# Second layer: the last two score tiles of the next head behind the projection instead of in front of it

## The reference

```python
qkv = xn @ w_qkv                      # x normalised, 256 -> 3 * 16 * 64
q = q * scale
sim = jnp.einsum('bhid,bhjd->bhij', q, k)
attn = jax.nn.softmax(sim, axis=-1)
out = jnp.einsum('bhij,bhjd->bhid', attn, v)
out = out.reshape(b, n, 1024) @ w_out
```

## Time and profile before

| | |
|---|---|
| median of the runs | 3472.14 us |
| the profiled execution | 3466.49 us, its span 3464.7 us |
| mean granted clock of the TensorE | 0.988 |
| busy share: PE, DVE, ACT, POOL | 96%, 72%, 56%, 68% |
| in the chain that ended last | PE 61%, every other engine 1% or less |
| phase B | from about 1239 us to the end |

### The profile page before, as it was taken

One profiled execution on the slowest core, in us unless ns is written; L12 is line 12 of the kernel. 1 busy time (PEld: TensorE's weight loads), 2 busy tenths in 40 slices (PEclk: granted clock), 3 DMA queues, 4 the chain that ended last, 5 costly groups with the idle time before them and its releaser, 6 DMA issues.

```text
span 3464.7 us, 58322 instructions
## 1 busy us (share of the span) xinstructions
PE 3327.1 (96%) x16386; PEld 2701.4 (78%) x16386; DVE 2480.8 (72%) x4709; ACT 1951.3 (56%) x3226; POOL 2359.6 (68%) x2084
## 2 busy tenths in 40 slices
PE   5999999999999969999999999999999999999997
PEld 4877777777777747888888888888888888888886
DVE  6877777777777756766766667667677666776764
ACT  3333333333333347767767777677777777767774
POOL 4666666666666527777777777777777777777776
PEclk9999999999999979999999999999999999999999
DMA  2110011001001032222222222222322222222222
GB/s 78 31 31 28 28 31 31 26 29 31 27 29 31 25 94 59 47 71 63 59 71 56 62 70 50 66 70 46 74 59 59 73 56 60 70 50 66 70 49 53
DMA packets 195099, 180.22 MB, mean 52 GB/s; under 512 B 87955, under 2 KB 155813, under 8 KB 194469
## 3 DMA queue, kind: packets, MB, share of 16 engines
q1 hardware_dynamic: 194980, 179.04, 20.7%
HBM read 77.25 MB, written 34.08 MB: 32 GB/s over the span
## 4 chain that ended last, share of the span: by engine, by line
PE 61%; DMA 1%; ACT 1%; DVE 1%; POOL 1%; issue 0%; SPq 0%; POOLq 0%; ACTq 0%; DVEq 0%
PE psV_b L1342 7%; PE psV_b L1347 7%; PE psS_b L1330 7%; PE psS_b L1329 7%; PE psV_b L1343 7%; PE psN_b L1315 6%; PE psY_b L1270 4%; PE psX_b L1270 4%; PE psY_b L1271 3%; PE psY_b L1272 3%; PE psX_b L1272 3%; PE psX_b L1271 3%; POOL pp_lo_b L1061 1%; PE psN_b L1399 0%; DMA xT_lo<-xT_lo_dram 0%
## 5 line engine op out<-in xcount | busy, mean ns | idle before, releaser
L1061 POOL TENSOR_TENSOR pp_lo_b<-pf_b,pp_hi_b 128x1024 fp32r<-128x1024 f32 x512 | 1227.6, 2398 | 606.6 <-ACT pp_hi_b L1103 518.9
L1206 DVE TENSOR_REDUCE negmax_b<-psN_b 128x2 fp32r<-128x1024 f32 x512 | 627.1, 1225 | 387.8 <-PE psN_b L1315 380.1
L1098 ACT ACTIVATE pf_b<-psS_b 128x1024 f32<-128x1024 f32 x512 | 526.0, 1027 | 239.4 <-PE psS_b L1330 236.2
L692 PE MATMUL psM_a<-wr_hi_a,xt_hi_a 128*128 128x512 f32 x1024 | 439.6, 429 | 48.1 <-DVE acc_a L528 40.1
L1329 PE MATMUL psS_b<-qA_b,kA_b 128*128 128x512 f32 x1024 | 405.6, 396 | 6.3 <-DVE qB_b L1221 4.5
L694 PE MATMUL psM_a<-wr_hi_a,xt_lo_a 128*128 128x512 f32 x1024 | 409.7, 400 | 0.0
L693 PE MATMUL psM_a<-wr_lo_a,xt_hi_a 128*128 128x512 f32 x1024 | 407.8, 398 | 0.0
L1330 PE MATMUL psS_b<-qB_b,kB_b 68*128 68x512 f32 x1024 | 406.4, 397 | 0.0
L1342 PE MATMUL psV_b<-pp_hi_b,vals_hi_b 128*128 128x512 f32 x1024 | 402.9, 393 | 1.4
L1343 PE MATMUL psV_b<-pp_hi_b,vals_lo_b 128*128 128x512 f32 x1024 | 402.3, 393 | 0.0
L1315 PE MATMUL psN_b<-kA_b,qA_b 128*128 128x512 f32 x1024 | 322.8, 396 | 4.8 <-DVE negmax_b L1206 4.1
(11 more groups left out here) (200 smaller groups left out, 7824.1 us busy)
## 6 DMA issues: line engine op xcount, KB each, us to landing
kA_b<-kA_b SPq DMA_DIRECT2D x128, 256.0 KB, 3.2
qB_b<-qA_b SPq DMA_DIRECT2D x128, 256.0 KB, 2.9
inverse_b<-inverse_dram SPq DMA_DIRECT2D x256, 128.0 KB, 3.0
x_a<-x_dram SPq DMA_DIRECT2D x64, 128.0 KB, 2.1
xT_hi_dram<-xrt_hi_a SPq DMA_DIRECT2D x64, 128.0 KB, 2.1
xT_lo_dram<-xrt_lo_a SPq DMA_DIRECT2D x64, 128.0 KB, 2.1
base_dram<-base_a SPq DMA_DIRECT2D x64, 128.0 KB, 1.8
xT_hi<-xT_hi_dram SPq DMA_DIRECT2D x16, 512.0 KB, 4.3
```

Source lines behind the costliest of these rows:

```text
L692: pe.matmul(out, lh, rh, start=start, stop=False)
L1061: pool.tensor_tensor(pp[1][:, c], pf[:, c], pp[0][:, c].bitcast(F32), ALU.subtract).then_inc(pl_pool, 1)
L1098: a.activation(pf[:, c], psS[:], ACT.Exp).then_inc(exp_act, 1)
L1206: v.tensor_reduce(negmax[:, n.slot(2), 2 * c:2 * c + 2], psN[:], AX.X, ALU.max, negate=True).then_inc(mx_dve, 1)
```

## The change

One call of two matmuls is moved on the TensorE's list, in every step: `scores(n, 1)` now stands behind the first projection of the step (queries in an even step, values or output in an odd one), and in front of `weigh(g, 0)`.

```diff
--- before.py
+++ after.py
@@ -1384,12 +1384,12 @@
                     weigh(m, 1)
                 if here:
                     scores_t(g, 1)
-                if n.within(0, NH):
-                    scores(n, 1)
                 if g.const % 2 == 0:
                     kq(g, q_unit(g), 1)
                 else:
                     shared(g)
+                if n.within(0, NH):
+                    scores(n, 1)
                 if here:
                     weigh(g, 0)
                 if n.within(0, NH):
```

## The result

The changed kernel takes 3630.01 us (median of 4 runs, 3628.53 to 3635.32), the kernel before in the same comparison 3472.43 us: 157.6 us more, ratio 1.0459, 95% interval [1.0441, 1.0477]. The forecast was 3600 us, range 3545 to 3670, slower.

The account below looks back on a forecast made before the run. TensorE's own list was taken to bound the head stage. Even 0.60 plus odd 0.47 made 1.07 us a pair, times 125 pairs 134 us, less 2 at the start: 3599, stated as 3600 us, range 3545 to 3670.

Parts of the forecast that it names:

- The mechanism: Head stage: moved pair releases second maximum, cast, low part and `row()` on VectorE, then the next step's first matmul; 3.7% slower.
- The prediction's other signs: Head stage: TensorE near 94% busy at clock 1.00, maxima waiting longer for psN, even casts near 0.9 us.
- The odd steps: Odd steps of the head stage: 0.63 us longer with a values' unit, 0.32 with an output unit, 0.47 on average.
- The wait of mt by itself: Mt waits about 0.2 us for the second maximum, swallowed by the larger wait for `row()`.
- The 1 to 2 us credited at the start: Start of the head stage: the values' projection runs inside the pair's 4.1 us wait for its maxima, gaining 1 to 2 us.
- the prediction's 4.27: Even step: chain from pair to the next step's second matmul takes 4.27 us; the TensorE has 3.59 us for it.
- the even step: Even step of the head stage: 0.68 us longer, 0.48 with the cast clear of GpSimd; taken as 0.60.
- The next instruction starts 0.08 us ahead of a cast's end.: VectorE in the even step: cast ends at 2412.86, next instruction starts at 2412.78, `row()` 0.61 us later.
- Everything up to otf moves forward, so I take 0.6.: Even step after an odd one that waited: ScalarE copies keys earlier relative to the TensorE; 0.6 us taken, not 0.68.
- A: Rival, head stage: only mt waits, 0.2 us a step, 50 us in all, 3517 us; chance 0.12.
- B: Rival, even steps: the cast stands fully behind a late otf, GpSimd's product; 3660 us; chance 0.14.
- C: Rival: not slower if the chain is no longer than the TensorE's 3.59 us; 4.1 us gained, 3468 by median; chance 0.05.

Follow-up runs that it names:

- the half move: Against the kernel before, the pair put between the third and fourth of the projection's six matmuls, three behind its old place; 3548.43 us, 1.0224.

## Why the prediction was right, and where it was off

The mechanism was right: a chain that goes from the pair through `row()` and back, longer than the work that the TensorE has left, and seen as a wait of the first psS matmul in nearly every step. The prediction's other signs came as well: the clock at 1.00, the maxima waiting longer for psN (2.44 us in the step shown, 0.89 before). The odd steps were well sized: by the TensorE's first matmuls they grew from 8.44 to 9.05 us with a values' unit and from 8.49 to 8.78 with an output unit (medians), 0.61 and 0.29 us against 0.63 and 0.32 forecast; over both kinds the mean is 0.42. The wait of mt by itself was put at 0.2 us; it shows alone in odd steps with `row()` first, 8.73 - 8.53 = 0.20 and 8.71 - 8.53 = 0.18 us. The 1 to 2 us credited at the start were 2.5.

That the chain of the step shown is 4.28 us, and the prediction's 4.27, is luck in part: its cast is 0.11 us shorter than forecast (0.77 for 0.88), and the first term below makes up for just that.

What was mis-sized is the even step, forecast at 0.60 us and measured at 0.87. Two terms of it failed:

1. "The next instruction starts 0.08 us ahead of a cast's end." In odd steps that holds (0.60 us behind the start of a cast of 0.68). In front of the query's low part there were 0.03 us behind the end instead, in all 104 even steps between 1500 and 3400 us (0.02 to 0.04). That is 0.11 us a step, 14 us. The trace of before has it, but not in the step that the prediction read: in 99 of 112 even steps there, that one among them, the low part started about 0.1 us behind the cast, right behind a copy of ScalarE. In the other 13 the copy was in time, and it is 1544.65 - (1543.48 + 1.14) = 0.03 us:

```profile
1543.48 1.14 DVE L1216 CAST pp_hi_b<-pf_b 128x1024 fp32r<-128x1024 f32 x1
...
1544.65 0.69 DVE L1195 SCALAR_TENSOR_TENSOR qA_b<-psX_b,qA_b 64x512 fp32r<-64x512 f32 x1
```

2. "Everything up to otf moves forward, so I take 0.6." Otf didn't always. The reciprocal is queued behind `row()` on VectorE; it feeds a DMA to DRAM and two back, and otf waits for these. The prediction listed what is queued behind the cast and left this one out. 32 of 104 otfs waited for the DMA; the casts of these steps are 1.30 us on the mean, those of the other 72 are 0.80. All even casts came to 0.96 us where 0.60 us of excess stood for a cast of about 0.80. That is 0.16 us a step, 20 us. Two kernels show the cause from two sides: with the reciprocal early the casts are 0.73 us and the time falls by 27 us; with otf cut short it falls by 29 us.

0.11 + 0.16 = 0.27 us is the difference of the even step; with 125 steps 34 us, less 6 for the odd steps (0.42 by the TensorE's starts against 0.47), 28 us. The excess was forecast at 134 - 2 = 132 us and measured at 158, 26 us short, so the two terms cover it. The other 4 of the 30 us between 3600 and 3630 are the forecast's own: its sum is 3599 us for the profiled execution, and with the 6 us that it names for the median it would have been 3605.

Of the rivals, A (only mt waits, 3517) fell with the changed kernel itself, and with `row()` first in odd steps, which made these 0.22 us shorter and left mt where it was. B (3660) had otf starting late, and that did happen, but in 32 of 104 steps and for another reason, the wait for the DMA; its longer form of 1.75 us did not come back (the median in the changed kernel is 1.29). C, not slower, holds where its condition holds: with the pair in the middle of the projection and the cast free of GpSimd, the time is that of before.

The cast's wait for GpSimd is what the Trainium skill ("SBUF — State Buffer", Who interferes with whom) states as an exclusive lock. The runs here agree: a cast that started inside a GpSimd product and had to wait ended 0.54 to 0.56 us behind that product's end, from 0.77 to 1.61 us long in the rows shown. The one of 1.61 us had run beside the product for 1.07 us and was then no nearer to its end than the one of 0.77 us, which had waited 0.22.

## What to carry to other kernels

When a step is moved on the engine that bounds the kernel, don't count the instructions that it passes; follow what it releases, through the in-order lists of the other engines, until it comes back, and compare that chain with the work left on the bounding engine between departure and return. Then look at what is queued behind the returning instruction too, small ones that feed a DMA above all: the reciprocal, 0.20 us long, cost some 26 us here by where it stood. And a cost that looks proportional to a move (78 us at half, 158 us at the whole) can be made of different things: at half it was all a cast held up by otf, in even steps alone; at the whole, the chain itself in all steps. The durations of single instructions tell them apart.

## What the runs showed of the hardware

A VectorE cast of 128 x 1024 is 0.68 us long alone and up to 1.83 us (in the half move) beside GpSimd products whose own length is 1.29 or 2.40 us; when and not only whether they meet decides. The other order is the same: otf started while a cast ran or waited ends 1.14 to 1.16 us behind the cast's end in most of the 110 such steps of the kernel before, where alone it takes 1.29. In the earlier trace rows this is its 1.75 us: the cast of the earlier trace rows ends at 2411.64 and otf at 2412.79. So of the two, the one that starts second has only 0.13 or 0.14 us of its own length to show for all the time beside the other.

VectorE's next instruction starts 0.08 us ahead of the cast's end or 0.03 us behind it. In these kernels it is 0.03 behind for the query's low part and for `row()`, which write from partition 64 on, and 0.08 ahead for the values' low part and the sum, which write from partition 0 on. That this is what makes the difference is not shown.

After a wait, the TensorE's first psS matmul starts 0.05 us behind the end of `row()`, and the second 0.33 to 0.35 us behind the first instead of 0.23, in all 173 such steps of the changed kernel; waits of this kind in nearly every step left the granted clock at 1.00.

And the same pair of matmuls costs nothing, 78 us or 158 us depending on whether it stands three or six matmuls later and on where the cast falls against a GpSimd instruction that no matmul of the stage waits for.
